# The first fill of a two-layer attention and feed-forward kernel: zeroing moved to GpSimd, split, and reordered

## The chip, the cores and the metric

The kernel runs on one core of one Trainium2 chip, with its five engines (TensorE, here PE; VectorE, DVE; ScalarE, ACT; GpSimd, POOL; SyncE, SP) and the DMA engines. The metric is the device time of one execution in microseconds (us), as the median of several runs. One execution was also profiled.

## What is computed

```python
x   # (128, 64, 128) float32: 128 sequences of 64 rows of width 128
x = x + _L0_xattn_ref(_layernorm(x), ctx, ctx, ...)   # normalised q, k and v, 16 heads of 8, sigmoid gate, output norm
x = x + _L0_ffn_ref(_layernorm(x), ...)               # gated feed-forward 128 -> 512 -> 512 -> 512 -> 128, ternary weights
x = x + _L1_xattn_ref(_layernorm(x), ctx, ctx, ...)   # 16 heads of 8, no gate
x = x + _L1_ffn_ref(_layernorm(x), ...)               # relu feed-forward 128 -> 512 -> 128
```

## The kernel before

The four parts run one after the other, and `x` stays in the core's memory (`x_res`). Attention works on units of 256 rows (two tiles of 128 rows, four sequences): 32 units in each layer. Every engine has its own hand-written program, a loop over steps j from -5 to N + 4, in which each engine works on several units at once: in step j it scores units j and j + 1, projects unit j + 2, turns unit j + 3, and normalises and measures units j + 4 and j + 5. Nothing reorders the instructions; only semaphores tie the engines together. So in steps -5 to 1 there is little work for TensorE, and its order there is a first fill of the pipeline. "Score(i, h)" below is one half of the first score products of unit i (L576). L579 and L562 are the second, shifted score products of a unit, from step 2 on.

For one unit the way is: DVE takes statistics (L952) and moments (L959); POOL makes `rstd` (L872, L873, L880); the rows are normalised (L968 on DVE for units 0 to 2; from unit 3 on L854 on POOL for x and L780 on ACT for the context, the latter with `ctx_bias`, POOL L886); PE turns them (L596); ACT copies the turned tile out (`take_turned`, L754); PE projects to q and k (`project`, L549 and L550, into the bank `ps_mid`); ACT copies these to `qk_t` (L741); four DMAs ("scatters", L534) bring them to `qk_sets`, for unit 0 two from ACT's queue and two from SP's, else all from SP's; PE scores (L576); DVE takes the row maxima (`highest`, L923) and splits them into three parts (L930 to L944); PE turns these (L662), ACT copies them (L794, `pieces`), and SP sends them to `shift`. The values go from `ps_mid` (L690) to `v_by_head` by ACT (L812). `ps_mid` holds one unit's projection or value at a time, so `project` of the next unit waits for L812 and for the gate's L817 behind it.

`qk_sets` has five slots for q and three for k, `v_by_head` has four for values. All must be zero outside the places that are written, so they are zeroed in the opening, each slot once: `clear_operands` on ACT (L305), `clear_values` on ACT (L313) for value slots 2 and 3, and a DVE memset (L363) for value slots 0 and 1. `value_ones` (L298) then writes columns of ones. `slots_cleared` counts what is zeroed.

`keep_streaming` (L332) issues matmuls on a blank tile whose result nobody reads, so that TensorE is not idle: "blanks" below. The table `FILL` says how many, by step and by place (0 is in front of `project`, 1 in front of the next score). Feed-forward weights are split into a high part on ACT (`w_hi`, L259) and a low part on DVE (`w_lo`, L269); `EARLY_SPLITS` says in which steps the first five groups are split.

## Time and profile before

| | |
|---|---|
| median of 3 runs | 953.3 us (950.07, 953.3, 954.53) |
| time of the profiled execution | 954.53 us |
| span of its profile | 952.7 us |
| PE busy | 918.2 us, 96% of the span |
| ACT, DVE, POOL busy | 772.2, 699.4, 325.6 us |
| mean granted TensorE clock | 0.998 of full speed |

The span runs from the first instruction to the last. What an engine does counts for the time only where the end of the chain of waits goes through it. Line numbers in the rows and in the text are those of the kernel before.

### The profile page before, as it was taken

Reading aid. Unit: us, or ns where it says so; the run is one execution under the profiler, and the core shown is the slowest. Engines: PE = TensorE matmul, PEld = TensorE weight load, DVE = VectorE, ACT = ScalarE, POOL = GpSimd, SP = SyncE. Lnnn points to the kernel's source line nnn. Section 1 sums busy time; section 2 is a strip of 40 time slices with the busy share of each in tenths; the row PEclk is TensorE's granted clock in tenths of the full one; section 3 lists DMA queues with packets and bytes.
Section 4 is the critical chain, followed back from the end, with each engine's and each line's share of the span. In section 5 each row is a group of like instructions: output and inputs, shape, how many; then the busy total and the mean of one; then the engine's idle time right before and its main releaser. Section 6 shows DMA issues by size and latency. Waiting matters only on the chain.

```text
span 952.7 us, 33022 instructions
## 1 busy us (share of the span) xinstructions
PE 918.2 (96%) x12342; PEld 712.8 (75%) x12349; DVE 699.4 (73%) x2046; ACT 772.2 (81%) x1409; POOL 325.6 (34%) x543
## 2 busy tenths in 40 slices
PE   6999999999989999999999999999999999999998
PEld 3687777787668888888788888767777777678886
DVE  7789998887776667666667666566766667589985
ACT  6798988889778988888888888667877777678985
POOL 5668888885530000000000000254444443021110
PEclk9999999999999999999999999999999999999999
DMA  6333322211000000000000000122222221100111
GB/s 210 94 102 96 103 76 84 75 49 45 5 1 1 1 0 0 0 0 0 0 0 0 0 0 1 56 82 74 73 63 65 67 68 54 25 2 34 44 45 56
DMA packets 54884, 41.72 MB, mean 44 GB/s; under 512 B 24416, under 2 KB 49248, under 8 KB 54752
## 3 DMA queue, kind: packets, MB, share of 16 engines
q1 hardware_dynamic: 53584, 37.12, 13.1%
q10 hardware_dynamic: 1168, 2.77, 0.8%
q8 instruction: 91, 1.49, 0.7%
q14 instruction: 41, 0.34, 0.1%
HBM read 16.79 MB, written 4.19 MB: 22 GB/s over the span
## 4 chain that ended last, share of the span: by engine, by line
PE 89%; DVE 4%; issue 3%; ACT 2%; DMA 1%; SPq 1%; ACTq 0%; POOL 0%; DVEq 0%; POOLq 0%
PE ps_w L1175 15%; PE ps_w L1174 15%; PE ps_w L579 7%; PE ps_av L634 6%; PE ps_w L576 5%; PE ps_w L562 4%; PE ps_mid L690 3%; PE ps_av L668 3%; PE ps_mid L549 3%; PE ps_y L677 3%; PE ps_mid L550 3%; PE ps_turn L644 2%; PE ps_turn L596 2%; PE g_ps_out L1174 2%; PE g_ps_out L1175 2%
## 5 line engine op out<-in xcount | busy, mean ns | idle before, releaser
L923 DVE TENSOR_REDUCE top<-ps_w 128x16 f32<-128x1024 f32 x128 | 155.9, 1218 | 94.6 <-PE ps_w L576 93.8
L1174 PE MATMUL ps_w<-g_h_lo,w_hi 128*128 128x512 f32 x512 | 206.7, 404 | 1.8 <-DVE g_h_lo L1429 1.7
L1175 PE MATMUL ps_w<-g_h_hi,w_hi 128*128 128x512 f32 x512 | 202.8, 396 | 0.0
L1429 DVE TENSOR_TENSOR g_h_lo<-g_h,g_h_hi 128x512 fp32r<-128x512 f32 x192 | 132.6, 690 | 87.2 <-ACT g_h_hi L1367 83.3
L133 POOL TENSOR_TENSOR front_rstd<-front_spread,minus_half 128x4 f32<-128x4 f32 x33 | 36.3, 1100 | 388.7 <-DVE front_spread L126 388.7
L733 ACT ACTIVATE prob_t<-ps_w 128x1024 f32<-128x1024 f32 x128 | 130.8, 1022 | 18.6 <-PE ps_w L579 18.0
L576 PE MATMUL ps_w<-qk_sets,qk_t 32*64 32x256 f32 x2048 | 143.9, 387 | 0.1
L1367 ACT ACTIVATE g_h_hi<-g_h 128x512 fp32r<-128x512 f32 x192 | 121.3, 632 | 18.6 <-DVE g_h L1439 14.4
L579 PE MATMUL ps_w<-qk_sets,qk_t 32*64 32x256 f32 x2048 | 134.2, 375 | 0.5 <-issue 0.5
L1174 PEld LDWEIGHTS ps_w<-g_h_lo,w_hi 128*128 128x128 f32 x512 | 96.7, 189 | 25.2 <-DVE g_h_lo L1429 3.5
L1175 PEld LDWEIGHTS ps_w<-g_h_hi,w_hi 128*128 128x128 f32 x512 | 96.9, 189 | 21.4
L1357 ACT ACTIVATE g_h<-ps_w,cols 128x512 f32<-128x512 f32 x128 | 87.2, 682 | 30.9 <-PE ps_w L1175 25.0
L854 POOL TENSOR_SCALAR normed<-x_res,moments,rstd 128x128 f32<-128x128 f32 x116 | 92.4, 803 | 40.0 <-PE ps_turn L596 36.1
L634 PEld LDWEIGHTS ps_av<-prob_t,v_by_head 128*32 128x32 f32 x4096 | 60.7, 110 | 30.2 <-issue 30.2
L579 PEld LDWEIGHTS ps_w<-qk_sets,qk_t 32*64 32x64 f32 x2048 | 75.2, 131 | 5.7 <-issue 1.6
L576 PEld LDWEIGHTS ps_w<-qk_sets,qk_t 32*64 32x64 f32 x2048 | 74.2, 131 | 5.6 <-issue 3.1
L634 PE MATMUL ps_av<-prob_t,v_by_head 128*32 128x64 f32 x4096 | 72.0, 221 | 4.5 <-issue 4.4
L741 ACT ACTIVATE qk_t<-ps_mid,qk_bias 128x256 f32<-128x256 f32 x128 | 53.6, 470 | 24.9 <-PE ps_mid L550 24.8
L880 POOL TENSOR_TENSOR rstd<-spread,minus_half 128x2 f32<-128x2 f32 (+2 forms) x62 | 61.3, 988 | 5.2
L812 ACT ACTIVATE v_by_head<-ps_mid 64x256 f32<-64x256 f32 x128 | 48.3, 377 | 13.7 <-PE ps_mid L690 9.1
L562 PE MATMUL ps_w<-shift,halves 32*64 32x512 bf16 x512 | 52.2, 398 | 2.0 <-DVE top L923 1.2
L1638 DVE TENSOR_TENSOR p_h_lo<-p_h,p_h_hi 128x512 fp32r<-128x512 f32 x64 | 42.7, 688 | 11.5 <-ACT p_h_hi L1620 10.4
(165 smaller groups left out, 2011.2 us busy)
## 6 DMA issues: line engine op xcount, KB each, us to landing
qk_sets<-qk_t SPq DMA_DIRECT2D x254, 64.0 KB, 1.9
ctx_in<-in_ctx SPq DMA_DIRECT2D x32, 128.0 KB, 3.0
ctx_in<-in_ctx_t SPq DMA_DIRECT2D x32, 128.0 KB, 2.6
out_x<-x_res SPq DMA_DIRECT2D x15, 256.0 KB, 2.0
x_res<-in_x SPq DMA_DIRECT2D x14, 256.0 KB, 3.7
shift<-pieces SPq DMA_DIRECT2D x128, 16.0 KB, 2.3
w_raw<-in_ff_weights SPq DMA_DIRECT2D x8, 256.0 KB, 3.6
w_raw<-in_ff_weights ACTq DMA_DIRECT2D x1, 768.0 KB, 9.1
```

The lines of the kernel that those rows point to most:

```text
L562: nc.tensor.matmul(ps_w[b * SEQ:(b + 1) * SEQ, g * 512:(g + 1) * 512], t.halves[rows, b, :], shift[rows, i % 2, :], start=True, stop=False)
L576: score = nc.tensor.matmul(out, qk_t[rows, unit % QKT, 0, at], qk_sets[rows, k_slot(unit), :, at], start=True, stop=True)
L579: shifted = nc.tensor.matmul(out, qk_t[rows, i % QKT, 1, at], qk_sets[rows, q_slot(i), :, at], start=False, stop=k == UNIT_TILES - 1)
L634: last = nc.tensor.matmul(ps_av[PAIR_COLS * c:PAIR_COLS * (c + 1), g * P + k * SEQ:g * P + (k + 1) * SEQ], t.v_by_head[:, i % UNROLL, k * ...
L733: nc.scalar.activation(prob_t[:, i % 2, 2 * half:2 * half + 2, :, :, :].rearrange("p g k m q -> p (g k m q)"), bank_pair(half), ACT.Exp).t ...
L854: last = nc.gpsimd.tensor_scalar(normed[:, i % 2, 0, k, :], t.x[:, span(i * UNIT_TILES + k, P)], moments[:, s, 0, k, 0:1], rstd[:, s, 0, k ...
L923: nc.vector.tensor_reduce(out=top[:, i % 2, half, :], in_=bank_pair(half).rearrange("p (a q) -> p a q", q=SEQ), op=ALU.max, axis=AX.X).the ...
L1174: nc.tensor.matmul(out, w_hi, x_lo, start=first and w_lo is None, stop=False)
L1175: return nc.tensor.matmul(out, w_hi, x_hi, start=False, stop=last)
L1357: nc.scalar.activation(h[:, o % 2, :], bank(o), ACT.Gelu, scale=t.s[:, 1 + level, o:o + 1]).then_inc(act_ready[level], 1)
L1367: nc.scalar.activation(h_hi[level][:, o, :], h[:, o % 2, :], ACT.Copy).then_inc(hi_ready[level], 1)
L1429: nc.vector.tensor_tensor(h_lo[level][:, o, :], h[:, o % 2, :], h_hi[level][:, o, :].bitcast(F32), ALU.subtract).then_inc(lo_ready[level], 1)
```

## The change

All of it is in the gated (first) attention and its opening. POOL zeroes all four value slots: three in one memset behind its other opening memsets, the fourth in step -3. The DVE memset and ACT's `clear_values` go. `value_ones` is called once for all four slots, in step -1. On DVE, unit 0 is normalised in front of the measuring of unit 1 instead of behind it. On ACT, a turned tile is copied before ACT issues its two scatters of unit 0. The four operand slots that ACT zeroed in step -1 are now zeroed one by one: two in step -1, one at the end of step -1, one at the end of step 0, and SP waits for each on its own. Two of the weight groups are split in steps 0 and 1 instead of -2. Four blanks that stood behind the wait for the biases now stand in front of it; blanks go from ten to three at place (-1, 1), and those at (0, 1) and (1, 1), four each, go.

```diff
-EARLY_SPLITS = {-3: range(0, 3), -2: range(3, 5)}
+EARLY_SPLITS = {-3: range(0, 3), 0: range(3, 4), 1: range(4, 5)}
...
-FILL = ({(-3, 0): 4, (-2, 0): 2, (-1, 0): 2, (-1, 1): 10, (0, 1): 4, (1, 0): 2, (1, 1): 4},
+FIRST_FILL = 4
+FILL = ({(-2, 0): 2, (-1, 0): 2, (-1, 1): 3, (1, 0): 2},
...
     clear_operands(nc, t, op, (FIRST_OPERANDS,))
-    clear_values(nc, t, op, slice(FIRST_SLOTS, UNROLL))
...
     nc.gpsimd.memset(t.shift[:, :, :], 0.0).then_inc(op.zeros_ready, 1)
+    nc.gpsimd.memset(t.v_by_head[:, 0:UNROLL - 1, :, :], 0.0).then_inc(op.values_cleared, 1)
...
     nc.tensor.matmul(op.ps[:, 3:4], op.wide[:, 2, :], t.cols[:, c["Wg"]:c["Wg"] + 1], start=True, stop=True).then_inc(op.bias_done, 1)
+    keep_streaming(nc, t, stream, FIRST_FILL)
     pe.wait_ge(op.chain, op.SCALED)
...
-    nc.vector.memset(t.v_by_head[:, 0:FIRST_SLOTS, :, :], 0.0).then_inc(op.chain, 1)
     dve.wait_ge(op.bias_done, 1)
...
-    value_ones(nc.vector, t, slice(0, FIRST_SLOTS))
+    dve.wait_ge(op.values_cleared, 2)
+    value_ones(nc.vector, t, slice(0, UNROLL))
...
+                if j < 0 and j + 3 >= READY:
+                    take_turned(j + 3)
                 if gated and j + 2 == 0:
                     act.wait_ge(qk_taken, 1)
                     scatter(act, 0, range(SETS // 2, SETS))
-                if j < 0 and j + 3 >= READY:
-                    take_turned(j + 3)
                 if gated and j == -1:
-                    clear_operands(nc, t, op, (slice(0, FIRST_OPERANDS.start), slice(FIRST_OPERANDS.stop, Q_SLOTS + K_SLOTS)))
+                    clear_operands(nc, t, op, (slot(q_slot(2)), slot(k_slot(2))))
...
+                if gated and j + 4 in (3, 4):
+                    clear_operands(nc, t, op, (slot(q_slot(j + 4)),))
...
+                if gated and j == -3:
+                    nc.gpsimd.memset(t.v_by_head[:, UNROLL - 1:UNROLL, :, :], 0.0).then_inc(t.opening.values_cleared, 1)
...
             def step(j):
+                if gated and j == -4:
+                    normalise(0)
...
-                    if j == 0:
-                        dve.wait_ge(op.slots_cleared, op.LATE_VALUES)
-                        value_ones(nc.vector, t, slice(FIRST_SLOTS, UNROLL)).then_inc(op.chain, 1)
...
-                    if gated and i == FIRST_SLOTS:
-                        sp.wait_ge(op.slots_cleared, op.LATE_OPERANDS)
+                    if gated and FIRST_SLOTS <= i < Q_SLOTS:
+                        sp.wait_ge(op.slots_cleared, op.FIRST_OPERANDS + i + 1 - FIRST_SLOTS)
```

ACT's order before, from its opening to the copy of q and k of unit 2:

```order
L305 ACTIVATE qk_sets<-blank 128x4096
L313 ACTIVATE v_by_head<-blank 128x1024 x2
L754 ACTIVATE turned<-ps_turn 128x512
L259 ACTIVATE w_hi<-w_raw 128x512 x3
L741 ACTIVATE qk_t<-ps_mid,qk_bias 128x256 x2
L534 DMA qk_sets<-qk_t 32x2x256 x2
L754 ACTIVATE turned<-ps_turn 128x512
L259 ACTIVATE w_hi<-w_raw 128x512 x2
...
L780 ACTIVATE normed<-ctx_in,ctx_bias,rstd 128x128 x2
...
L305 ACTIVATE qk_sets<-blank 128x3072
...
L812 ACTIVATE v_by_head<-ps_mid 64x32x8 x2
L817 ACTIVATE gate_exp<-ps_mid,gate_nb 128x2
```

The same stretch of the changed kernel, whose own line numbers are a few smaller or larger:

```order
L311 ACTIVATE qk_sets<-blank 128x4096
L752 ACTIVATE turned<-ps_turn 128x512
L264 ACTIVATE w_hi<-w_raw 128x512 x3
L739 ACTIVATE qk_t<-ps_mid,qk_bias 128x256 x2
L752 ACTIVATE turned<-ps_turn 128x512
L532 DMA qk_sets<-qk_t 32x2x256 x2
...
L778 ACTIVATE normed<-ctx_in,ctx_bias,rstd 128x128 x2
...
L311 ACTIVATE qk_sets<-blank 128x1024 x2
L808 ACTIVATE v_by_head<-ps_mid 64x32x8 x2
L813 ACTIVATE gate_exp<-ps_mid,gate_nb 128x2
L311 ACTIVATE qk_sets<-blank 128x1024
...
L264 ACTIVATE w_hi<-w_raw 128x512
```

The value clears are gone, the copy of the second turned tile (L752) stands in front of the DMAs, two weight splits have left, and half of the operand clearing stands in front of the first value copy (L808), the rest behind it.

DVE's order before, from the biases of the opening to the normalising of unit 1:

```order
L363 MEMSET v_by_head 128x2048
L365 TENSOR_TENSOR open_sums<-ps_y,cols 128x1
...
L373 TENSOR_SCALAR qk_bias<-open_sums 128x1
L952 BN_STATS stats<-x_res 128x6 x2
L952 BN_STATS stats<-ctx_in 128x6 x2
L959 BN_AGGR moments<-stats 128x2 x4
L968 TENSOR_SCALAR normed<-x_res,moments,rstd 128x128 x2
L968 TENSOR_SCALAR normed<-ctx_in,moments,rstd 128x128 x2
```

In the changed kernel, over the same stretch:

```order
L362 TENSOR_TENSOR open_sums<-ps_y,cols 128x1
...
L370 TENSOR_SCALAR qk_bias<-open_sums 128x1
L968 TENSOR_SCALAR normed<-x_res,moments,rstd 128x128 x2
L968 TENSOR_SCALAR normed<-ctx_in,moments,rstd 128x128 x2
L952 BN_STATS stats<-x_res 128x6 x2
L952 BN_STATS stats<-ctx_in 128x6 x2
L959 BN_AGGR moments<-stats 128x2 x4
```

The memset is gone, and the four L968 of unit 0 have passed the measuring of unit 1.

PE's order before, from the projection of unit 2 (step 0) to the first shifted product:

```order
L549 MATMUL ps_mid<-turned,wa 128x256
L332 MATMUL ps_av<-blank 128x512 x4
L576 MATMUL ps_w<-qk_sets,qk_t 64x256 x8
L662 MATMUL ps_turn<-ident,top_parts 128x128
L339 MATMUL ps_y<-wa,y 128x128 x2
...
L332 MATMUL ps_av<-blank 128x512 x2
...
L332 MATMUL ps_av<-blank 128x512 x4
L576 MATMUL ps_w<-qk_sets,qk_t 64x256 x8
...
L562 MATMUL ps_w<-shift,halves 64x512 x4
```

And now:

```order
L547 MATMUL ps_mid<-turned,wa 128x256
L574 MATMUL ps_w<-qk_sets,qk_t 64x256 x8
L660 MATMUL ps_turn<-ident,top_parts 128x128
L337 MATMUL ps_y<-wa,y 128x128 x2
...
L330 MATMUL ps_av<-blank 128x512 x2
...
L574 MATMUL ps_w<-qk_sets,qk_t 64x256 x8
...
L560 MATMUL ps_w<-shift,halves 64x512 x4
```

The two groups of four blanks between a projection and the next score are out; the rest stands as it stood.

## Rows read from the trace of the kernel before

**Rows 1.** The page: the span, and part 4, the chain that ended last, by engine.

```profile
span 952.7 us, 33022 instructions
...
PE 89%; DVE 4%; issue 3%; ACT 2%; DMA 1%; SPq 1%; ACTq 0%; POOL 0%; DVEq 0%; POOLq 0%
```

**Rows 2.** The chain in order of time, opening: start us, us, what.

```profile
21.50 2.64 ACT qk_sets L305
```

**Rows 3.** Timeline of PE, opening: start us, us, what, idle before and releaser.

```profile
6.37 0.56 PE L325 MATMUL ps_y<-cols,y 128*128 128x1 f32 x2
9.12 1.89 PE L332 MATMUL ps_av<-blank 128*128 128x512 bf16 x4 [2.19 <-DVE qk_bias L373]
...
26.18 0.67 PE L549 MATMUL ps_mid<-turned,wa 128*128 128x256 f32 x2 [1.07 <-ACT gate_exp L817]
...
27.34 0.81 PE L332 MATMUL ps_av<-blank 128*128 128x512 bf16 x3
28.08 1.09 PE L576 MATMUL ps_w<-qk_sets,qk_t 32*64 32x256 f32 x16
...
32.56 0.59 PE L549 MATMUL ps_mid<-turned,wa 128*128 128x256 f32 x2
...
33.42 1.03 PE L332 MATMUL ps_av<-blank 128*128 128x512 bf16 x4
34.38 1.09 PE L576 MATMUL ps_w<-qk_sets,qk_t 32*64 32x256 f32 x16
```

**Rows 4.** Timeline of DVE, opening.

```profile
2.00 0.78 DVE L348 CAST ident<-ident 128x128 bf16<-128x128 f32 x1
...
6.44 1.76 DVE L363 MEMSET v_by_head<- 128x2048 f32 x1 [0.38 <-issue]
...
8.92 0.15 DVE L373 TENSOR_SCALAR qk_bias<-open_sums 128x1 f32<-128x1 f32 x1
...
10.17 0.57 DVE L968 TENSOR_SCALAR normed<-x_res,moments,rstd 128x128 f32<-128x128 f32 x2
...
13.71 1.90 DVE L269 TENSOR_TENSOR w_lo<-w_raw,w_hi 128x512 fp32r<-128x512 f32 x3 [0.25 <-ACT w_hi L259]
...
20.79 0.21 DVE L382 COPY y<-cols 128x128 f32<-128x128 f32 x1
...
34.85 0.18 DVE L944 SCALAR_TENSOR_TENSOR top_parts<-top_parts,rest 128x32 bf16<-128x32 bf16 x1
```

**Rows 5.** Timeline of POOL, opening.

```profile
1.75 0.95 POOL L292 MEMSET shift<- 128x1024 bf16 x1
...
6.58 1.03 POOL L880 TENSOR_TENSOR rstd<-spread,minus_half 128x4 f32<-128x4 f32 x1
...
10.88 1.01 POOL L880 TENSOR_TENSOR rstd<-spread,minus_half 128x4 f32<-128x4 f32 x1
...
16.88 0.19 POOL L872 TENSOR_SCALAR spread<-moments 128x2 f32<-128x2 f32 x1 [2.80 <-DVE moments L959]
...
18.53 1.00 POOL L886 TENSOR_SCALAR ctx_bias<-moments,rstd 128x1 f32<-128x1 f32 x2
19.51 2.07 POOL L854 TENSOR_SCALAR normed<-x_res,moments,rstd 128x128 f32<-128x128 f32 x2
```

**Rows 6.** DMA issues, 2.1 to 2.58 us; KB each, last column us to landing.

```profile
w_raw<-in_ff_weights ACTq DMA_DIRECT2D x1, 768.0 KB, 9.1
```

**Rows 7.** Timeline of ACT, opening.

```profile
9.53 1.99 ACT L313 ACTIVATE v_by_head<-blank 128x1024 f32<-128x1024 bf16 x2
...
20.14 0.87 ACT L780 ACTIVATE normed<-ctx_in,ctx_bias,rstd 128x128 f32<-128x128 f32 x2
...
21.39 3.71 ACT L305 ACTIVATE qk_sets<-blank 128x3072 f32<-128x3072 bf16 x2
```

**Rows 8.** DMA issues, 30.15 to 30.5 us, the last scatter of unit 2.

```profile
qk_sets<-qk_t SPq DMA_DIRECT2D x1, 64.0 KB, 3.2
```

**Rows 9.** Windows: us, busy (x) of PE, PEld, DVE, ACT, POOL, then PEclk, DMA share, GB/s.

```profile
9.00:11.00 2.00, 1.88 (x4) 0.43 (x4) 1.97 (x13) 2.00 (x3) 0.51 (x3) 1.00 0.97 286
```

More of the change, by code:

```diff
@@ L194, in k_slot, with slot @@
     return Q_SLOTS + i % K_SLOTS
+def slot(n):
+    return slice(n, n + 1)
 class Opening:
@@ L213, in __init__ @@
         self.slots_cleared = sem("slots_cleared")
+        self.values_cleared = sem("values_cleared")
         self.chain = sem("chain")
@@ L219, in __init__ @@
         self.late_x = sem("late_x")
-    COUNTED, WIDENED, CLEARED, BIASED, SCALED, VALUE_WIDE, LATE_ONES = 1, 2, 3, 4, 5, 6, 7
+    COUNTED, WIDENED, BIASES_COPIED, BIASED, SCALED, VALUE_WIDE = 1, 2, 3, 4, 5, 6
     BLANK, SHIFT = 2, 3
-    FIRST_OPERANDS, LATE_VALUES, LATE_OPERANDS = 1, 2, 3
+    FIRST_OPERANDS = 1
 def load_x(t, eng, n):
@@ L306, in clear_operands, with open_tensor @@
     last.then_inc(op.slots_cleared, 1)
-def clear_values(nc, t, op, slots):
-    wide = t.v_by_head[:, slots, :, :].rearrange("p s h c -> p s (h c)")
-    width = UNIT_TILES * HEADS * PAIR_COLS
-    for s in range(FIRST_SLOTS):
-        last = nc.scalar.activation(wide[:, s, :].rearrange("p (a n) -> p a n", n=512),
-                                    t.blank[:, :].unsqueeze(1).to_broadcast([P, width // 512, 512]), ACT.Copy)
-    last.then_inc(op.slots_cleared, 1)
-def open_tensor(nc, t, op, pe):
+def open_tensor(nc, t, op, pe, stream):
     c = COLS
@@ L361, in open_weights @@
     nc.vector.tensor_tensor(t.gate_col[:, :], c["Wg"], c["ln_q_g"], ALU.mult)
-    nc.vector.tensor_copy(t.qk_bias[:, 1, 1:2], c["b_k"])
-    nc.vector.memset(t.v_by_head[:, 0:FIRST_SLOTS, :, :], 0.0).then_inc(op.chain, 1)
+    nc.vector.tensor_copy(t.qk_bias[:, 1, 1:2], c["b_k"]).then_inc(op.chain, 1)
     dve.wait_ge(op.bias_done, 1)
@@ L701, in run @@
                 if gated:
-                    open_tensor(nc, t, op, pe)
+                    open_tensor(nc, t, op, pe, ps_av[:, :])
                 for j in range(-5, N + 5):
@@ L805, in step @@
                         act.wait_ge(op.chain, op.VALUE_WIDE)
-                    if gated and i == FIRST_SLOTS:
-                        act.wait_ge(op.chain, op.LATE_ONES)
                     act.wait_ge(v_done, i + 1)
@@ L1097, in step @@
                     front_normalise(nc, t, front, dve, 2, 0)
-                if max(READY, NORMALISED) <= j + 4 < EARLY_UNITS:
+                if max(READY, NORMALISED) <= j + 4 < EARLY_UNITS and j > -4:
                     normalise(j + 4)
@@ L1145, in step @@
                         sp.wait_ge(op.slots_cleared, op.FIRST_OPERANDS)
-                    if gated and i == FIRST_SLOTS:
-                        sp.wait_ge(op.slots_cleared, op.LATE_OPERANDS)
+                    if gated and FIRST_SLOTS <= i < Q_SLOTS:
+                        sp.wait_ge(op.slots_cleared, op.FIRST_OPERANDS + i + 1 - FIRST_SLOTS)
                     sp.wait_ge(qk_taken, i + 1)
```

## The prediction

> **What bounds the kernel now.** I read the page first, then the chain in order of time, then the timelines of PE, ACT, DVE and POOL over the first 40 us. PE holds 89% of the chain that ended last [rows 1]. From step 2 on (about 37 us) PE hardly waits, so whatever the opening saves shifts the rest of the program by the same amount, and the change can be worth no more than the opening holds. In the opening the chain leaves PE: a piece of it is ACT zeroing operand slots [rows 2], and PE's projection of unit 2 begins at 26.18 behind an idle 1.07 that ACT's L817 ended [rows 3]. Then blanks stand in PE's order between projection and score. So I work out when three marks would be reached: projection of unit 2 (26.18), of unit 3 (32.56), and the end of the row maxima parts of unit 1 (34.85 + 0.18 = 35.03) [rows 3, 4].
>
> **The change part by part.**
>
> *The memset leaves DVE.* It runs 6.44 to 8.20; the bias sums behind it wait for bias products that PE ended at 6.37 + 0.56 = 6.93 [rows 3, 4]. So these sums can begin at 7.0. From 8.20 their chain went on to 8.92 + 0.15 = 9.07, seven short operations in about 0.95, counting the overlap of starts; so they end at 7.95.
>
> *POOL takes the zeroing.* A GpSimd memset over 1024 elements a partition took 0.95 [rows 5]. Three slots have 3072 elements: three times that is 2.85, less two fixed starts, so 2.65 to 2.85. It stands behind the shift memset (ends 2.70) and ends at 5.35 to 5.55. POOL's next work, `rstd` of unit 0, could not start before 6.05, since L872 and L873 stand in front of the L880 at 6.58 [rows 5]. Hidden, with 0.5 to spare. If the float32 tile cost twice as much an element (no row here shows a wide float32 memset on POOL), it would end near 8.2 and delay `rstd` by 2.2: that is a rival below. The fourth slot (0.95) stands behind `rstd` of unit 2, near 13.5 to 14.4, and the next moments come at 16.1: nothing.
>
> *Unit 0 normalised sooner.* `rstd` of unit 0 is there at 6.58 + 1.03 = 7.61 [rows 5]. DVE begins at 7.95 instead of 10.17 [rows 4]: 2.2 sooner. Then the measuring of unit 1 starts at 9.0, which is where it was (9.07). So the 2.2 us reach PE's first turning, ACT's first copy and the projection of unit 0, but not unit 1: its `rstd` still ends at 10.88 + 1.01 = 11.89 [rows 5]. DVE has by then done the measuring of unit 2, too, and normalises unit 1 from 11.95 to 13.05. The w_lo splits start at 13.05 instead of 13.71 [rows 4]; their high parts are ready, since ACT is free from 10.9, and the 768 KB of weights land at 2.14 + 9.1 = 11.2 [rows 6]. DVE is from here on 0.65 ahead, and so are the moments of unit 3, on which POOL's L872 at 16.88 waited [rows 5]: now 16.2.
>
> *ACT: value clears, weight splits and scatters.* The value clears (1.99 [rows 7]) ended at 11.5, before the first turned tile came; with the tile 2.2 sooner they would be late, without them they are not. Taking two weight splits out of step -2 (a split of that size takes DVE 1.90 / 3 = 0.63 [rows 4], ACT about as much) and copying the turned tile ahead of two DMA issues make ACT ready for `normed` of unit 3 (L780) by about 18.0. That instruction then waits for POOL: 16.2 and the same way as before (16.88 to 18.53) gives `ctx_bias` from 17.85; its two operations took 1.00 while DVE ran a two-input w_lo split beside them, which is now over; 0.5 to 1.0 gives 18.4 to 18.85. L780 started at 20.14 [rows 7], so it is **1.3 to 1.7 sooner; I take 1.7.**
>
> *Operand clears.* Before, 3.71 from 21.39, and the first value copy stood behind them [rows 7]. Now two clears of 1024 elements stand there; two of that size took 1.99 [rows 7]. **Saved: 1.7.** The third (about 1.0) starts behind L817, when PE projects unit 2 (27.34 - 26.18 = 1.16 [rows 3]); ACT would wait for that projection anyway. It is hidden, but by 0.2 only. The fourth lies beside the projection of unit 3, the same way.
>
> So the projection of unit 2 begins at 26.18 - 1.7 - 1.7 = 22.8.
>
> *Blanks.* Four at (0, 1) held the score back by 28.08 - 27.34 = 0.74, four at (1, 1) by 34.38 - 33.42 = 0.96 [rows 3]. The seven taken out at (-1, 1) are worth at most 7 x 0.26 = 1.8 on PE, but PE waits for ACT there (the 1.07 of idle time), so nothing is gained by them. The four moved in front of the bias wait end at about 8.8, before the first tile to turn at 9.1: nothing. After the first group, the score of unit 1 begins 3.4 + 0.74 = 4.15 sooner, at 23.95; the projection of unit 3 the same 4.15 sooner. **0.74 counts in full.**
>
> *What is late next.* The second group would give 4.15 + 0.96 = 5.1 by PE alone. But the row maxima of unit 1 and their parts, ended at 35.03 [rows 4], follow the score of unit 1's second half, only 4.15 sooner: they end at 30.9. Before, PE came for them at 34.38 + 1.09 = 35.45, so they had 0.4 of slack; with it the gain is at most 4.55. The score of unit 2 needs its scatters too: they start when q and k of unit 2 are copied, 3.4 sooner like its projection, and the last landed at about 30.2 + 3.2 = 33.4 [rows 8], so now at 30.0 at the latest, against 34.38: a gain of 4.4 at most. **Of the 0.96 only 0.2 to 0.25 counts.** The w_hi and w_lo splits put into steps 0 and 1 (0.63 each) fall on ACT before it copies `pieces`, where the turned parts are there at 25.2 and PE wants the result at 26.7: ACT ends it at 26.45, hidden by 0.25; on DVE they stand behind a maximum and in front of nothing that PE wants within 0.6.
>
> *Sum.* 1.7 + 1.7 + 0.74 + 0.2 = 4.35. At its low ends (1.3, 1.6, 0.7, 0) it is 3.6; the high end is 4.4 by the scatters, or 5.1 if scatters and maxima were no bound. Against the profiled execution: 954.53 - 4.35 = 950.2, its span 952.7 - 4.35 = 948.35. That execution is the slowest of the three; off the median of 953.3 the sum leaves 948.95. I forecast **949.0 us**, 0.45% less. A measurement of this kernel can tell about 0.5% (4.8 us) from no change, so the forecast lies just inside.
>
> **A rule against this change.** DVE's CAST of 128x128 started at 2.00 and took 0.78, while 128x128 operations nearby take 0.2 to 0.3; it ended at 2.78, and POOL's memset that ran beside it ended at 1.75 + 0.95 = 2.70 [rows 4, 5]. POOL now has the memset of 2.65 us right behind. On the other side, DVE's COPY at 20.79 took 0.21 in the midst of POOL's L854, 19.51 to 21.58 [rows 4, 5], and the L354 of the opening is a copy of the same kind, a column spread over 128 elements. So I cost the copy at nothing, and the cast too if it slips in between the two memsets. The Trainium skill (SBUF — State Buffer, under "SBUF: two separate sides", Who interferes with whom) says that a DVE copy or cast in a 2-port mode and a GpSimd instruction exclude each other for the whole instruction; for the cast the trace agrees with its 0.78.
>
> **The rivals.**
>
> 1. *DVE is locked out until POOL's long memset ends.* If the cast doesn't get in between the memsets, it ends at about 5.4 to 5.6; the copy, statistics and moments of unit 0 (4.21 to 5.96 before) end at 7.0, and `rstd` of unit 0 at 8.65. Unit 0 is normalised at 8.7 instead of 7.95; all that hangs on the moments of unit 1 is 0.75 later: gain 3.6, 949.7 us. For it: the cast's 0.78. Against: it ended 0.08 behind a memset, so it gets in as soon as one ends. Chance 0.13.
> 2. *The float32 memset costs twice as much.* `rstd` of unit 0 at 9.8, DVE 1.85 behind the forecast: gain 2.5, 950.8 us. Nothing in the trace speaks for it. With other short waits of that size, such as a clear or a split that is hidden here by 0.2 and isn't: chance 0.15.
> 3. *The gain isn't there, or is given back* (the profile shows a new wait in step 2 or 3, of DVE's maxima or SP's scatters, that uses up more than 3 us): 952.5 us, chance 0.07.
> 4. *TensorE's clock.* Slower than before. Blanks of 512 columns start 0.43 apart at 9.12, and about 0.22 apart at 27.34 [rows 3]: that is 1.2 and 2.4 GHz, though the granted clock of 9 to 11 us reads 1.00 [rows 9]. Fifteen blanks in steps -1 to 1 are gone, and PE would sit idle from 21.6 to 22.8. If the clock fell back there, or rose much later than now, each us of PE work would cost nearly another; PE has some 12 us of work up to the first shifted product. The gain is used up at 4.5 us of work at half the clock, and the kernel is over 0.5% slower from 9.5 us on: 958 us. Against it: the idle 1.07 in front of 26.18 didn't lower it before (the projection behind it took 0.67), and real work fills the rest. The Trainium skill (TensorE: Matmul & The Clock Gate, Part 1) says that half rate is the default and that activity lifts it; a short gap like this one is no return by the trace. Chance 0.04.
> 5. *More than 0.5% faster.* Not another mechanism: the bound of 4.4 is only 0.4 from the limit of 4.8, the three runs before lie 4.5 us apart, and if scatters and maxima don't bind, the gain is 5.1: 948.2 us. Chance 0.28.
>
> The forecast itself, gain 3.8 to 4.7, has what is left, 0.33, on the side of no measurable change.
>
> **How the numbers follow.** Faster by over 0.5%: case 5, and 0.02 of the others, 0.30. Slower by over 0.5%: case 4 and a mishap of the measurement, 0.05. The rest, 0.65: the forecast, cases 1 to 3. The likeliest time is 949.0. Cases 1 and 2 reach 950.8, case 3 952.5; case 5 948.2, and the medians of three runs move by 1.5 us either way. 946.5 to 952.6 leaves out case 4, half of case 3 and the tails: 2 in 10.
>
> **What would show it.** In the changed profile: DVE's first L968 at 7.95 (10.17); POOL's memset of 2.65 to 2.85 behind the shift memset; DVE's cast at 0.8 or less (rival 1: over 3); L780 of unit 3 at 18.4 to 18.9; the projection of unit 2 near 22.8 and of unit 3 near 28.4; the score of unit 2 near 30.0 with a short wait in front, for a DMA or DVE; the parts of unit 1's maxima ended near 30.9. It would be wrong if blanks or projections at 14 to 25 us took twice their warm time (clock), or if the marks were met and the span was not 4 us shorter: then something later than step 2 sets the end.

## The result: 0.45% slower

| | before | changed |
|---|---|---|
| median (20 executions each) | 952.17 us (949.33 to 957.68) | 956.28 us (951.01 to 962.42) |
| ratio | | 1.0045, interval 1.0029 to 1.0061 |
| profiled execution, its span | 954.53, 952.7 us | 953.59, 951.1 us |
| PE busy | 918.2 us | 915.1 us |
| time around the span, median | 1.8 us | 2.5 us |

The time around the span is the device time less the span; for the kernel before it is that of its executions beside the experiments below. The forecast was 949.0 us in a range of 946.5 to 952.6. The median lies 7.3 above the forecast, on the other side of no change. The profiled execution is a quick one of its kernel, 1.6 us shorter in its span than the one of before: alone it would have told the wrong story. Line numbers from here on are those of the kernel that a row belongs to.

The changed kernel's page, span and chain, against [rows 1]:

```profile
span 951.1 us, 32991 instructions
...
PE 89%; DVE 5%; issue 3%; ACT 1%; SPq 1%; DMA 1%; POOL 0%; DVEq 0%; POOLq 0%; ACTq 0%
```

ACT has lost one point of the chain and DVE has won one. The timeline of DVE in the opening, against [rows 4]:

```profile
2.00 3.37 DVE L346 CAST ident<-ident 128x128 bf16<-128x128 f32 x1
3.86 1.58 DVE L352 COPY y<-cols 128x128 f32<-128x128 f32 x1
...
8.37 0.59 DVE L968 TENSOR_SCALAR normed<-x_res,moments,rstd 128x128 f32<-128x128 f32 x2
```

And of POOL, against [rows 5]:

```profile
2.63 2.66 POOL L298 MEMSET v_by_head<- 128x3072 f32 x1
...
14.02 0.95 POOL L888 MEMSET v_by_head<- 128x1024 f32 x1
16.54 0.19 POOL L870 TENSOR_SCALAR spread<-moments 128x2 f32<-128x2 f32 x1 [1.58 <-DVE moments L959]
...
18.21 0.53 POOL L884 TENSOR_SCALAR ctx_bias<-moments,rstd 128x1 f32<-128x1 f32 x2
```

The long memset took 2.66 us, as forecast, and float32 costs here what bfloat16 does: 1024 elements take 0.95 in L888 and in the shift memset of [rows 5]. But the cast stood in the memset to its end: 3.37 instead of 0.78, and the copy behind it 1.58 instead of 0.23. Unit 0 is normalised at 8.37, not at 7.95 (10.17 before). POOL's L870 for unit 3 is 0.34 sooner, its `ctx_bias` 0.32. The timeline of ACT, against [rows 7]:

```profile
18.78 0.88 ACT L778 ACTIVATE normed<-ctx_in,ctx_bias,rstd 128x128 f32<-128x128 f32 x2 [1.92 <-POOL ctx_bias L884]
...
20.04 1.99 ACT L311 ACTIVATE qk_sets<-blank 128x1024 f32<-128x1024 bf16 x2
22.67 0.77 ACT L808 ACTIVATE v_by_head<-ps_mid 64x256 f32<-64x256 f32 x2 [0.64 <-PE ps_mid L688]
```

ACT is 1.36 sooner at L778 and its clears are 1.7 shorter, both inside the forecast's bounds. Then the first value copy, which had always stood behind the clears, waits 0.64 for PE. Why PE is late is in its own timeline, against [rows 3]:

```profile
15.39 0.59 PE L548 MATMUL ps_mid<-turned,wa 128*128 128x256 f32 x2
17.53 1.06 PE L594 MATMUL ps_turn<-ident,normed 128*128 128x128 f32 x4 [1.54 <-DVE normed L968]
18.39 1.49 PE L330 MATMUL ps_av<-blank 128*128 128x512 bf16 x3
19.80 1.68 PE L574 MATMUL ps_w<-qk_sets,qk_t 32*64 32x256 f32 x16
...
23.87 0.67 PE L547 MATMUL ps_mid<-turned,wa 128*128 128x256 f32 x2 [0.27 <-ACT gate_exp L813]
...
26.48 0.23 PE L660 MATMUL ps_turn<-ident,top_parts 128*128 128x128 bf16 x1 [0.49 <-DVE top_parts L944]
...
34.26 0.41 PE L560 MATMUL ps_w<-shift,halves 32*64 32x512 bf16 x4
```

Its windows there (the columns are those of [rows 9]):

```profile
15.00:20.00 5.00, 3.46 (x15) 1.83 (x19) 4.50 (x27) 2.06 (x5) 3.20 (x7) 0.76 0.52 162
20.00:25.00 5.00, 4.73 (x48) 2.86 (x48) 2.53 (x3) 3.99 (x7) 3.75 (x8) 0.90 0.16 53
```

PE is idle for 1.54 us, and behind that the granted clock falls from 2.4 to 1.2 GHz: four turnings take 1.06 (those of unit 1 took 0.66 at 13.51), and 16 score products 1.68, where their next group, at 22.50, took 1.09. The projection of unit 2 comes at 23.87, 2.3 sooner and not 3.4; the first shifted product at 34.26 (36.95 before), 2.7 sooner. In this execution the fall was short, and of the 2.7 the span kept only 1.6. So one profile alone could not settle it.

### The profile page after: what moved, and what is told of

The parts are those of the page before. It is cut to its first block, busy times and chain, and to the rows that moved or that the text cites. A ratio compares the mean times of both kernels' runs of the same rounds, so it can differ in the third digit from the quotient of the medians.

```text
span 951.1 us, 32991 instructions
## 1 busy us (share of the span) xinstructions
PE 915.1 (96%) x12328; PEld 710.8 (75%) x12334; DVE 698.3 (73%) x2043; ACT 770.3 (81%) x1409; POOL 328.3 (35%) x545
## 4 chain that ended last, share of the span: by engine, by line
PE 89%; DVE 5%; issue 3%; ACT 1%; SPq 1%; DMA 1%; POOL 0%; DVEq 0%; POOLq 0%; ACTq 0%
PE ps_w L1174 15%; PE ps_w L1173 15%; PE ps_w L577 7%; PE ps_av L632 7%; PE ps_w L574 5%; PE ps_w L560 4%; PE ps_mid L688 3%; PE ps_av L666 3%; PE ps_y L675 3%; PE ps_mid L547 3%; PE ps_mid L548 2%; PE ps_turn L642 2%; PE ps_turn L594 2%; PE g_ps_out L1173 2%; PE g_ps_out L1174 2%
## 5 line engine op out<-in xcount | busy, mean ns | idle before, releaser
L808 ACT ACTIVATE v_by_head<-ps_mid 64x256 f32<-64x256 f32 x128 | 48.3, 377 | 13.8 <-PE ps_mid L688 9.2
```

## The experiments

The theories at this point. **A:** the missing blanks let TensorE's clock fall in the opening, for long in some executions, and this costs more than the opening gains. **B:** the loss is "the port", which stands here for the prediction's rule against this change: DVE held off by POOL's memset. Theory B of the forecasts for e1, e2 and e4 is wider, any part of the change but the blanks. **C:** DVE's new order (unit 0 normalised before unit 1 is measured) is worth nothing. "Mark" below is the start of the second group of value products (50.64 in the kernel before); a minus means sooner. "Stops" is PE's idle time between 60 and 240 us, in the profiled execution, that no releaser in the profile ended; it is read under e4 and e11, and no theory had it. Ratios are to the kernel before on the same chip, with the interval at 95%.

| kernel | median us | ratio | interval | mark | stops us | clock of 0.993 or less |
|---|---|---|---|---|---|---|
| changed, e4, e11 | 956.28, 954.49, 953.84 | 1.0045, 1.0042, 1.0042 | 1.0015 to 1.0070 | -2.53, +3.67, -4.21 | 4.5, 3.5, 5.4 | 18 of 44 |
| e1: old blanks | 948.61 | 0.9983 | 0.9966 to 1.0000 | -2.46 | 0 | 0 of 12 |
| e2: before, new blanks alone | 960.05 | 1.0117 | 1.0085 to 1.0148 | +6.7 | 3.0 | 5 of 6 |
| e3: memset behind cast | 957.38 | 1.0091 | 1.0065 to 1.0116 | +1.65 | 2.0 | 5 of 6 |
| e5: seven blanks back | 952.21 | 0.9998 | 0.9982 to 1.0015 | -1.23 | 2.5 | 0 of 12 |
| e6: eight blanks back | 952.15 | 0.9997 | 0.9977 to 1.0016 | -1.55 | 3.2 | 0 of 12 |
| e7: all back but the first four | 949.49 | 0.9983 | 0.9964 to 1.0003 | -2.55 | 0.4 | 0 of 12 |
| e8: e1, memset behind `rstd` | 950.81 | 0.9997 | 0.9980 to 1.0015 | -1.09 | 0 | 0 of 12 |
| e9: e7, memsets in gaps | 948.71 | 0.9968 | 0.9953 to 0.9983 | -3.28 | 0 | 0 of 12 |
| e10: e9, seven of ten blanks | 949.68 | 0.9978 | 0.9964 to 0.9993 | -3.68 | 0.9 | 0 of 12 |
| e12: e7, DVE's old order | 948.63 | 0.9978 | 0.9961 to 0.9996 | -2.71 | 0.2 | 0 of 12 |

The last column counts executions whose mean granted clock over the whole span was 0.993 or less. The first row's interval runs from the lowest to the highest bound of e4 and e11; that of the changed kernel lies inside. The kernel before, run beside them, has medians of 950.72 (e1 to e4), 951.82 (e5 to e8) and 951.40 (e9 to e12), and a clock of 0.993 or less in 2 of 93 executions. Its own profile has no stops.

### e1: the change with the old blanks

```diff
-FIRST_FILL = 4
-FILL = ({(-2, 0): 2, (-1, 0): 2, (-1, 1): 3, (1, 0): 2},
+FIRST_FILL = 0
+FILL = ({(-3, 0): 4, (-2, 0): 2, (-1, 0): 2, (-1, 1): 10, (0, 1): 4, (1, 0): 2, (1, 1): 4},
```

> The changed kernel with all the blanks of before in their old places (28 instead of 11 in the opening), everything else as changed. Theory A (clock): the executions of the changed kernel at 957 to 962 us are those with a mean granted clock of 0.986 to 0.991, PE's clock having fallen in the opening behind its idle times, and the missing blanks let it. Then with the blanks back every execution has a clock of 0.996 or more and the median is 949 to 951 us, 1 to 3 us under before. Theory B (the rest of the change, say the order on DVE and ACT, makes the long executions): the spread stays, some executions at a clock under 0.992, median 955 to 957 us.

With the blanks back the loss is gone, and the mark is 2.5 us sooner. The median ratio of 0.9983 is a small gain whose interval reaches no change. So the rest of the change, port and all, doesn't lose: B alone falls. (The blanks that the changed kernel has in the opening are 13, 4 + 2 + 2 + 3 + 2, and not the 11 of the forecast.)

### e2: the kernel before, with only the blanks changed

```diff
-FILL = ({(-3, 0): 4, (-2, 0): 2, (-1, 0): 2, (-1, 1): 10, (0, 1): 4, (1, 0): 2, (1, 1): 4},
+FIRST_FILL = 4
+FILL = ({(-2, 0): 2, (-1, 0): 2, (-1, 1): 3, (1, 0): 2},
...
+    keep_streaming(nc, t, stream, FIRST_FILL)
```

> The kernel before with only the blanks changed: four in front of the bias wait, three at (-1, 1), none at (0, 1) and (1, 1). Theory A: part of the executions at a clock under 0.992, the others about 1.5 us faster than before (0.74 + 0.96 less), median between 950 and 957 us, with a spread of 8 us or more. Theory B: no execution under 0.992, median 950.5 to 951.5 us.

1.2% slower, more than theory A had: the median of 960.05 lies above its 950 to 957, and none of the six was faster than the median of before, the one with a mean clock of 0.994 (959.11) included. Its timeline of PE, then its windows:

```profile
22.25 1.09 PE L578 MATMUL ps_w<-qk_sets,qk_t 32*64 32x256 f32 x16
25.93 0.95 PE L551 MATMUL ps_mid<-turned,wa 128*128 128x256 f32 x2 [2.59 <-ACT gate_exp L819]
...
27.67 1.98 PE L578 MATMUL ps_w<-qk_sets,qk_t 32*64 32x256 f32 x16
```

```profile
25.00:30.00 5.00, 4.07 (x23) 2.18 (x24) 2.05 (x12) 2.45 (x8) 3.29 (x7) 0.62 0.02 6
30.00:35.00 5.00, 5.00 (x32) 3.79 (x31) 1.16 (x3) 1.87 (x6) 1.42 (x2) 0.50 0.30 72
...
45.00:50.00 5.00, 5.00 (x69) 3.68 (x73) 4.10 (x14) 4.06 (x9) 1.42 (x3) 0.83 0.21 71
```

Without its seven blanks PE has nothing for 2.59 us. The clock falls behind that gap, and stays down for some 20 us although PE is busy nearly without a break: the same 16 products take 1.98 instead of 1.09. A slow PE that is always busy doesn't look like a wait in any list of waits; only the clock's column and the time of one instruction show it. This is A, without any other part of the change. But the 1.2% is not the price of the clock alone: this profile has 3.0 us of stops too.

### e3: POOL's long memset behind DVE's cast

```diff
+    pool.wait_ge(op.chain, op.COUNTED)
     nc.gpsimd.memset(t.v_by_head[:, 0:UNROLL - 1, :, :], 0.0).then_inc(op.values_cleared, 1)
```

> The changed kernel, but GpSimd's memset of three value slots waits until DVE's cast of the identity (L346) is done. Shared-port theory: the cast is back at 0.78 us; if the spread copy L352 does not take the port, it runs 0.2 us at about 4.2 in the midst of the memset, the moments of unit 0 end at 5.96 and the first normalising starts at 7.95 instead of 8.37; the first shifted product starts about 0.4 to 0.7 earlier. If the copy takes the port it ends with the memset, at 5.5, and nothing is gained. The time of the whole keeps the two groups by clock in either theory A or B (median 953 to 957), unless the shorter idle time of PE (1.54 us in front of the turning at 17.53) keeps the clock up.

Its DVE and POOL in the opening:

```profile
2.00 0.78 DVE L347 CAST ident<-ident 128x128 bf16<-128x128 f32 x1
3.96 1.62 DVE L353 COPY y<-cols 128x128 f32<-128x128 f32 x1 [1.18 <-DMA cols<-in_cols]
```

```profile
2.83 2.66 POOL L299 MEMSET v_by_head<- 128x3072 f32 x1
```

The cast is free again, and now the copy is held: it began at 3.96 and ended at 5.58, 0.09 behind the memset's end at 2.83 + 2.66 = 5.49. Only its mark matters for the port, and the clock drowned it: low in 5 of 6 executions, and in the profiled one at half for some 14 us, from a little after 23. So the time, 0.9% slower, says nothing of the port, and the rows do.

### e4 and e11: the changed kernel, profiled again

No edit in either; each gave 12 executions more and another profile.

> The changed kernel as it is, once more, on this chip. Both theories: median 954 to 958 us, executions in two groups, 950 to 955 at a clock of 0.996 or more and 957 to 962 at 0.986 to 0.991. If the profiled execution falls into the second group, theory A expects its low clock between 13 and 45 us; theory B between 240 and 330 us or behind 850.

> The changed kernel once more, beside the two above on the same chip. Theory A: 4 to 6 of 12 executions with a mean clock under 0.992 and 7 us longer than the rest, median 1.003 to 1.006 of before; a clock fall near 17.5 or 23 us in the profiled execution.

The timeline of PE in e4's profile, then its windows:

```profile
17.55 0.82 PE L594 MATMUL ps_turn<-ident,normed 128*128 128x128 f32 x4 [1.56 <-DVE normed L968]
...
19.58 1.98 PE L574 MATMUL ps_w<-qk_sets,qk_t 32*64 32x256 f32 x16
...
25.41 1.22 PE L547 MATMUL ps_mid<-turned,wa 128*128 128x256 f32 x2
```

```profile
20.00:25.00 5.00, 5.00 (x40) 3.06 (x32) 1.23 (x1) 3.36 (x7) 3.81 (x8) 0.50 0.17 54
...
35.00:40.00 5.00, 4.67 (x34) 3.14 (x31) 3.83 (x14) 2.24 (x7) 1.44 (x4) 0.66 0.16 59
```

And of PE in e11's profile:

```profile
17.55 0.66 PE L594 MATMUL ps_turn<-ident,normed 128*128 128x128 f32 x4 [1.55 <-DVE normed L968]
18.05 0.81 PE L330 MATMUL ps_av<-blank 128*128 128x512 bf16 x3
...
23.15 0.67 PE L547 MATMUL ps_mid<-turned,wa 128*128 128x256 f32 x2 [1.16 <-ACT gate_exp L813]
...
31.27 0.23 PE L660 MATMUL ps_turn<-ident,top_parts 128*128 128x128 bf16 x1 [0.47 <-DVE top_parts L944]
...
32.86 0.41 PE L560 MATMUL ps_w<-shift,halves 32*64 32x512 bf16 x4
```

Three profiles of one program, with the same gap of 1.54 to 1.56 us in front of the same turning: in one the clock stayed, in one it fell for some 3 us, in one for some 20. With it the mark lies at -4.21 or at +3.67, 7.9 us apart. So such a gap doesn't force the fall. e11's median, and its 4 executions under 0.992, came as forecast; a fall in its profiled execution was forecast too and didn't come. Over the 44 executions, the 18 with a mean clock of 0.993 or less have a median span of 956.6 us, and the 26 others 950.55.

Those 26 are no faster than the kernel before, and e11's profile shows why. With the clock up, its mark is 4.21 us sooner, and its span only 2.0 shorter. These are PE's waits without a releaser ("issue") between 60 and 240 us, with their sum, number and longest, in e11, then in e7 (below), then PE's timeline in e11:

```profile
PE ps_av L632 <- issue: 4.8, 5, 1.2
PE ps_turn L642 <- issue: 0.6, 1, 0.6
```

```profile
PE ps_av L632 <- issue: 0.4, 1, 0.4
```

```profile
105.40 0.33 PE L632 MATMUL ps_av<-prob_t,v_by_head 128*32 128x64 f32 x9 [0.97 <-issue]
...
127.97 0.32 PE L632 MATMUL ps_av<-prob_t,v_by_head 128*32 128x64 f32 x7 [1.17 <-issue]
...
151.12 0.31 PE L632 MATMUL ps_av<-prob_t,v_by_head 128*32 128x64 f32 x5 [1.12 <-issue]
```

In e11 PE stops in every third unit, mostly for about 1 us, in the midst of the 64 value products, with 9, 7, 5 products left, then 3 and 1. The changed kernel's two other profiles stop at the same places of the program, though not at all of them. In e5, e6 and e10, which have 7, 8 and 12 blanks more, the stops come with just as many products more left: at 151.57, 151.71 and 191.06 with 12, 13 and 13, where the changed kernel has 5, 5 and 1. Counted in the traces, the stops over 0.2 us stand 1024 PE instructions apart, or a multiple of that. So they hang on the count of PE's instructions and not on a wait for another engine; that the supply of instructions is what runs short is my reading and wasn't tested. The kernels with 13 blanks lose 2.0 to 5.4 us to them, those with 20 or 21 lose 2.5 and 3.2, those with 25 or 28 at most 0.9. e2 differs from the kernel before in its blanks only, and has 3.0 where that has none. By these profiles taking blanks out cost twice, and the second time far behind the opening.

### e5, e6, e7: which blanks

```diff
-FILL = ({(-2, 0): 2, (-1, 0): 2, (-1, 1): 3, (1, 0): 2},
+FILL = ({(-2, 0): 2, (-1, 0): 2, (-1, 1): 10, (1, 0): 2},                            # e5
+FILL = ({(-2, 0): 2, (-1, 0): 2, (-1, 1): 3, (0, 1): 4, (1, 0): 2, (1, 1): 4},       # e6
+FILL = ({(-2, 0): 2, (-1, 0): 2, (-1, 1): 10, (0, 1): 4, (1, 0): 2, (1, 1): 4},      # e7
```

> The changed kernel with the seven blanks at place (-1, 1) back (ten instead of three), which stand where PE otherwise waits for ACT and cost nothing on the path; nothing at (0, 1) and (1, 1). Theory A1 (the clock is lost in the idle time up to the projection of unit 2, which these seven fill): no execution with a mean clock under 0.992, median 947 to 949 us, 1 us under the kernel with all old blanks. Theory A2 (what counts is the work in steps 0 and 1 or the idle time in front of the turning at 17.5): still a part of the executions at 0.986 to 0.991, median 951 to 957 us.

> The changed kernel with the four blanks at (0, 1) and the four at (1, 1) back, three left at (-1, 1). Theory A1: low clocks stay, median 953 to 957 us. Theory A2: no execution under 0.992, median 948 to 950 us.

> The changed kernel with all later blanks back and only the first four still in front of the bias wait. Against the kernel with all blanks in their old places it tells what moving the first four does. Both theories: no execution under 0.992, median 948 to 949.5 us, as that one. The time around the span was about 1.8 us there and 2.2 to 3.4 us in every kernel with the first four moved: if moving them is what makes that, it is 2.2 to 3.4 us here, and the median is 1 us higher; if the low clock or the missing blanks make it, it is 1.8 us.

Either group is enough against the long falls: 0 of 12 each. But the kernel is only back at the time of before: both medians (952.21, 952.15) lie above what their forecasts gave for a clock that holds (947 to 949, 948 to 950), and e7, run beside them, is 2.7 us faster. Neither stopped a short one: each has two windows of 5 us with a granted clock of 0.80 and 0.86 (15 to 25 us in e5, 20 to 30 in e6), and e7's opening has none. At the mark that is 1.3 and 1.0 us against e7; the stops are 2.5 and 3.2 us against 0.4. Both groups together are e7, and its ratio is that of e1 (0.9983; 949.49 and 948.61 us): the four blanks moved in front of the bias wait show no effect, as forecast. What the eight cost, e7's timeline of PE shows:

```profile
25.66 1.09 PE L574 MATMUL ps_w<-qk_sets,qk_t 32*64 32x256 f32 x16
26.68 0.23 PE L660 MATMUL ps_turn<-ident,top_parts 128*128 128x128 bf16 x1
```

In the changed kernel the score stands at 24.90, 0.76 sooner, but L660 then waits 0.49 for DVE's `top_parts` and comes at 26.48, 0.20 sooner. So in that execution most of what the eight blanks took was handed to a wait for DVE.

### e8, e9: where POOL's memset stands

e8, from e1: the three slots are zeroed behind `rstd` of unit 0.

```diff
-    nc.gpsimd.memset(t.v_by_head[:, 0:UNROLL - 1, :, :], 0.0).then_inc(op.values_cleared, 1)
...
+                if gated and j == -5:
+                    nc.gpsimd.memset(t.v_by_head[:, 0:UNROLL - 1, :, :], 0.0).then_inc(t.opening.values_cleared, 1)
```

> All blanks in their old places, and GpSimd's memset of three value slots moved behind the rstd of unit 0. Shared-port theory: cast 0.78 us and copy 0.2 us again, moments of unit 0 at 5.96, bias sums at 7.0; the memset then runs about 7.7 to 10.3. If the tensor_scalar operations of DVE (weights by a column, the first normalising) take the port, they stop until 10.3 and unit 0 is normalised later than the 8.4 of the changed kernel; if not, it is normalised at 7.95, and the whole is 0.4 us faster than with the memset in front: median 947.5 to 949 us. No execution under a clock of 0.992 in either case.

e9, from e7: slot 0 behind the cast, slot 1 behind the copy, the other two in step -3.

```diff
-    nc.gpsimd.memset(t.v_by_head[:, 0:UNROLL - 1, :, :], 0.0).then_inc(op.values_cleared, 1)
+    pool.wait_ge(op.chain, op.COUNTED)
+    nc.gpsimd.memset(t.v_by_head[:, 0:1, :, :], 0.0)
+    pool.wait_ge(op.chain, op.WIDENED)
+    nc.gpsimd.memset(t.v_by_head[:, 1:2, :, :], 0.0).then_inc(op.values_cleared, 1)
...
-                    nc.gpsimd.memset(t.v_by_head[:, UNROLL - 1:UNROLL, :, :], 0.0).then_inc(t.opening.values_cleared, 1)
+                    nc.gpsimd.memset(t.v_by_head[:, 2:UNROLL, :, :], 0.0).then_inc(t.opening.values_cleared, 1)
```

> All later blanks in their old places (the first four moved), and GpSimd zeroes one value slot behind DVE's cast, one behind DVE's spread copy, and the last two in one memset behind the rstd of unit 2, so that no operation of DVE that takes the shared port meets a memset. Shared-port theory: cast 0.78 us, copy 0.2 us, unit 0 normalised from 7.6 (8.4 in the changed kernel, 10.2 before), everything that hangs on the moments of unit 1 about 0.7 us sooner: the value products of unit 1, which started 2.5 us sooner than before with the memset in front, now start 3.0 to 3.3 sooner, no execution under a clock of 0.992, ratio 0.9965 to 0.998. If the port were not what held DVE, nothing moves against the kernel with the memset in front.

DVE and POOL in e8:

```profile
7.60 2.76 DVE L969 TENSOR_SCALAR normed<-x_res,moments,rstd 128x128 f32<-128x128 f32 x2
```

```profile
7.45 2.76 POOL L887 MEMSET v_by_head<- 128x3072 f32 x1
```

The two normalisings, 0.59 elsewhere, end at 10.36 behind the memset's end at 10.21: these too are held off, and the mark is 1.4 later than in e1. DVE and POOL in e9:

```profile
2.00 0.78 DVE L349 CAST ident<-ident 128x128 bf16<-128x128 f32 x1
3.85 0.23 DVE L355 COPY y<-cols 128x128 f32<-128x128 f32 x1 [1.07 <-DMA cols<-in_cols]
...
7.64 0.59 DVE L971 TENSOR_SCALAR normed<-x_res,moments,rstd 128x128 f32<-128x128 f32 x2
```

```profile
2.83 0.95 POOL L299 MEMSET v_by_head<- 128x1024 f32 x1
4.14 0.95 POOL L301 MEMSET v_by_head<- 128x1024 f32 x1 [0.35 <-DVE y L355]
```

In pieces that fit DVE's waits for its DMAs, the memsets cost DVE nothing: L971 at 7.64 instead of 8.37, and the mark 0.73 sooner than in e7. By its interval e9 is 0.2 to 0.5% faster than before, the lowest ratio of all; e7's interval overlaps it, so only the marks tell these two apart.

### e10: three blanks fewer, with room

e9 with `(-1, 1): 7`.

> The same with seven instead of ten blanks at (-1, 1). In the kernel with ten, ACT waited 0.52 us for the value product of unit 0 behind them, with three it did not. Theory A (enough of the work is left to hold the clock): no execution under 0.992, and another 0.4 to 0.6 us of gain: value products of unit 1 3.5 to 3.8 us sooner than before, ratio 0.996 to 0.9975. If three blanks less already let the clock go in part of the executions, the median is above that of the kernel with ten.

The mark is 0.4 sooner, as forecast, the median 1 us later, the intervals overlap: inconclusive between the two. No execution had a low mean clock, and the stops are 0.9 us against none.

### e12: DVE's order undone

From e7: `normalise(0)` stands behind the measuring of unit 1 again, as in the kernel before.

```diff
-                if gated and j == -4:
-                    normalise(0)
...
-                if max(READY, NORMALISED) <= j + 4 < EARLY_UNITS and j > -4:
+                if max(READY, NORMALISED) <= j + 4 < EARLY_UNITS:
```

> The changed kernel with all later blanks back, and DVE normalising unit 0 behind the measuring of unit 1 again, as before. Theory C (the order on DVE is worth nothing for unit 1 and later, which wait for rstd of unit 1): unit 0 is turned 1.2 us later, but rstd of unit 1 comes 1.1 us sooner and the value products of unit 1 start within 0.3 us of the kernel with the new order; ratio about 0.9985. Theory D (the new order is what makes the gain): they start 1 us or more later, ratio 0.9995 or more.

PE's first turning comes 1.2 later than in e7 (10.84 against 9.63), and the mark is not later but 0.16 sooner than e7's: theory C holds. DVE in e12, then in e7:

```profile
11.81 0.57 DVE L968 TENSOR_SCALAR normed<-x_res,moments,rstd 128x128 f32<-128x128 f32 x2
```

```profile
12.35 0.60 DVE L968 TENSOR_SCALAR normed<-x_res,moments,rstd 128x128 f32<-128x128 f32 x2 [0.50 <-POOL rstd L878]
```

This is unit 1. In the new order it waits for its `rstd`, because its moments come behind the normalising of unit 0. What unit 0 wins, unit 1 pays, and the later units hang on the second.

## Why the prediction was wrong, step by step

- **The step that failed is rival 4, the clock**, held at a chance of 0.04 and at nothing in the sum. Its mechanism happened: with the blanks out, the clock fell behind idle stretches of PE, and 18 of 44 executions have a mean clock of 0.993 or less. What I held against it was "the idle 1.07 in front of 26.18 didn't lower it before". One gap in one execution, with ten blanks at 19.65 ahead of it and four behind its projection, was taken for what any gap of that length does. In the changed kernel the clock fell behind a gap of 1.54 to 1.56, in e3 behind one of 1.15 and in e2 behind one of 2.59, and not in every execution. I had costed the fifteen blanks by what they take from PE, never by what they hold up.
- **The place was another.** I looked for the idle stretch in front of the projection of unit 2 (21.6 to 22.8). In both profiles of the changed kernel with a fall it came behind the gap in front of unit 2's turning, at 17.5, which no term has. In e2 and e3, and for a short time in e6, it came in front of the projection.
- **The trace of before held such a fall all along**, in the feed-forward part, outside the 40 us that I read. These are windows of PE alone (us, busy, PEclk, DMA share, GB/s):

```profile
265.00:270.00 5.00, 3.21 (x10) 0.97 0.00 0
270.00:275.00 5.00, 5.00 (x18) 0.69 0.00 0
```

There PE was idle for 0.30, 0.72 and 0.72 us within some 3 us (three waits for DVE's `g_h_lo`), and the clock then stood at half for some 3 us. So "a short gap like this one is no return by the trace" was not so even there.
- **The price:** 958 against 956.28 is near by luck. The measured median lies between two groups: in device time, 959.9 for the 18 executions with a low mean clock and 953.2 for the other 26. I took 12 us of work up to the first shifted product as what half clock could touch; in e4 and e2 the fall lasted some 20 us, and in e2 it ran 4 us past that product (42.71).
- The Trainium skill's rule that I quoted (TensorE: Matmul & The Clock Gate, Part 1) is that half rate is the default and activity lifts it. The 0.50 behind the gaps in e2 and e4 agrees with its first half. With the second it is only in part so: PE was busy nearly without a break for some 20 us in both before the clock rose.
- **"Whatever the opening saves shifts the rest" is the second step that failed.** It held within 0.7 us where the stops are at most 0.4: the median span of e1, e7, e8, e9 and e12 is 2.1, 2.3, 1.0, 2.7 and 2.8 us under that of the kernel before beside it, the marks are 2.5, 2.6, 1.1, 3.3 and 2.7 sooner. It failed where blanks are missing: e5 and e6 have marks 1.2 and 1.6 sooner and median spans 0.3 us longer, e10 has 3.7 sooner and 1.8 shorter. In the changed kernel the stops of PE between 60 and 240 us took 3.5 to 5.4 us, as much as the opening had saved. Rival 3 had such a giving back at 0.07, but looked for it in step 2 or 3, as a wait for DVE or SP.
- **Rival 1, the port, happened too**, at a chance of 0.13. The forecast leaned on a COPY at 20.79 that took 0.21 "in the midst of" L854. That row is two instructions back to back; the copy started 1.28 behind the row's start, and the first of the two had ended 0.03 before (19.51 + 1.24 = 20.75), so it may well lie between them, as I had allowed the cast to. e3 and e8 show copies and normalisings held off to the end of a memset. The cast did not get in between two memsets that stand back to back. It was priced at 0.75; e9 against e7 gives 0.73 (marks -3.28 and -2.55). The rule of the Trainium skill (SBUF — State Buffer, Who interferes with whom) was right, and this case's 3.37 and 1.62 us agree with it.
- **Rival 2** did not happen: 2.66 us for 3072 elements of float32.
- **Unit 0 sooner:** 8.37 for 7.95. Without the port (e9) it is 7.64: the bias sums began at 6.72 there and not at 7.0, so the port cost 0.73 and not the 0.42 that the two figures differ by. That the order doesn't help unit 1 stood in the text; e12 shows that it doesn't help the mark either.
- **ACT, 1.7 and 1.7:** 1.36 (in its range of 1.3 to 1.7, at the low end, since the port held POOL's inputs back) and 1.7. Of this 3.06, only 2.3 reached the projection of unit 2, because PE at half clock came 0.64 late with the value product. With the clock kept (e11) it was 26.18 - 23.15 = 3.03, where I had 3.4 and 2.9 at the low ends: the sum up to here held when the clock does.
- **Blanks, 0.74 and 0.2, DVE next:** in e11 the first shifted product comes at 32.86, 4.09 sooner, where the terms give 4.35. The bound by DVE's maxima was seen rightly: L660 waits 0.47 for `top_parts` there. The seven blanks at (-1, 1) were not free, as I had them: with them (e7) ACT waits 0.52 for the value product behind them, and the projection of unit 2 comes at 23.77, 0.62 later than in e11.

**Open.** The 26 executions of the changed kernel without a low mean clock have a median span of 950.55, and e7 has 947.7. The profiles account for that: e11 is 1.66 ahead of e7 at the mark, has 5.0 us more of stops, and its span is 2.9 longer. But they are single executions, and no run changed the stops by themselves, say with instructions that do nothing. What makes the stops short with 28 blanks isn't shown. The time around the span is 2.4 to 3.2 us in the median of all kernels with 13 blanks (changed, e2, e3, e4, e11), and 1.8 to 1.9 in all others. e7 has the first four moved as well and shows 1.8, so it isn't that. It is 0.7 us of the 4.1 lost, and I have no cause for it. Nor do I know what decides whether a given execution's clock falls, and for how long.

## What to carry to other kernels

Fillers on TensorE have two prices, the time that they take and the clock that they hold: before taking any out, find the longest idle stretch that then stands in a thinly filled part, and price half clock behind it (here some 20 us) with a chance from many executions, not from one profile. They also shift all that stands behind them in PE's program, so after any change in their number look for idle time without a releaser over the whole span, not only where the fillers were. Work moved to GpSimd is free only beside VectorE work that it doesn't lock out, so cut it into pieces that fit VectorE's waits. And bringing the first unit sooner was worth nothing here, where the second unit paid for it.

## What the runs showed of the hardware

- The granted clock fell behind idle stretches of TensorE of 1.15 to 2.59 us in the opening (changed, e2 to e6), and in the kernel before behind three of 0.30 to 0.72 us within some 3 us, at 269.7. Other executions of the same program didn't fall (e11, 1.55 and 1.16 us). At half clock PE stayed busy and the clock still didn't come back for some 20 us (e2, e4) or 14 (e3); in the changed kernel's first profile, e5 and e6 it was back after 3.4. The mean clock was 0.993 or less in 18 of 44 executions of the changed kernel; with either group of blanks back, none of the 96 of e1, e5 to e10 and e12 was under 0.994.
- TensorE stops for up to 1.5 us without a releaser, at places 1024 of its instructions apart or a multiple of that (e11: 105.40, 127.97 and on, every 22 to 23 us; also the changed kernel, e2 to e6, e10).
- The column of the granted clock can't be trusted before the first rise: it reads 1.00 over 5 to 10 us in every profile, while in the changed kernel four blanks at 7.28 take 1.87 us, and in e11 three at 18.05 take 0.81.
- A GpSimd memset takes 0.95 us for 1024 elements a partition, bfloat16 or float32, and 2.66 to 2.76 for 3072 of float32. While it runs, a DVE cast, a copy of a spread column and a `tensor_scalar` by a column wait to its end (3.37, 1.62 and 2.76 us for 0.78, 0.23 and 0.59). DVE's statistics do not: in e9 they take 0.49 us at 4.45, inside the memset of 4.14 to 5.09.
